# A new order of the steps in the cycle of the last part, on four engines

## What is computed

```python
# L3_xattn, for each of 64 sequences; x is layer-normed, textual = ctx (77 keys x 128)
txt_proj = textual @ Ws                     # 77 x 128
feat_proj = x @ W                           # 128 x 128
h = tanh(txt_proj[None] + feat_proj[:, None] + b)     # 128 tokens x 77 keys x 128
rho = h @ w + mask                          # 128 x 77
att = softmax(rho)
txt_h = att @ textual
out = tanh(txt_h @ Wcw.T + bcw) * x + tanh(txt_h @ Wcb.T + bcb)
# L3_ffn: each token to one of 8 experts, at most 1024 tokens for each, in order of tokens
probs = softmax(x @ wg); idx = argmax(probs)
locations = running count of the tokens of the same expert
mask = onehot(idx) * (locations < 1024)
out = gate * (x @ W[idx].T + b[idx])
```

## Time and profile before

| what | us |
|---|---|
| median of 3 runs (3680.53 to 3686.89) | 3683.99 |
| the profiled execution | 3685.05 |
| its span in the trace | 3683.3 |
| from 2708.45 to 3598.20, 56 turns of the last part | 889.75 |

### The profile page before, as it was taken

One profiled execution on the slowest core, in us unless ns is written; L12 is line 12 of the kernel. 1 busy time (PEld: TensorE's weight loads), 2 busy tenths in 40 slices (PEclk: granted clock), 3 DMA queues, 4 the chain that ended last, 5 costly groups with the idle time before them and its releaser, 6 DMA issues. The chain is left out here.

```text
span 3683.3 us, 79834 instructions
## 1 busy us (share of the span) xinstructions
PE 3112.4 (85%) x28490; PEld 2223.3 (60%) x28490; DVE 2687.1 (73%) x7707; ACT 2309.9 (63%) x6401; POOL 778.5 (21%) x1179
## 2 busy tenths in 40 slices
PE   6999999999997797899999949565388888888887
PEld 5666666666664465566666634225266676666675
DVE  2777777777774344788888856995578888888885
ACT  2889898989894353444444410420378888788885
POOL 0223232323232000233333300000122212222121
PEclk9999999999996898899999969777678888788887
DMA  1011111111110211011111100002100000000000
GB/s 40 19 32 32 31 31 32 31 32 30 33 32 13 74 43 37 19 28 28 28 28 28 26 16 0 0 0 72 31 10 12 13 13 13 13 12 13 13 13 8
DMA packets 173531, 90.21 MB, mean 24 GB/s; under 512 B 43971, under 2 KB 169541, under 8 KB 173156
## 3 DMA queue, kind: packets, MB, share of 16 engines
q1 hardware_dynamic: 160612, 72.67, 7.2%
q0 software_dynamic: 4096, 8.40, 0.7%
q10 hardware_dynamic: 8448, 4.20, 0.4%
HBM read 42.86 MB, written 42.34 MB: 23 GB/s over the span
## 5 line engine op out<-in xcount | busy, mean ns | idle before, releaser
L2149 DVE TENSOR_TENSOR th<-tf 128x2048 f32<-128x2048 f32 x256 | 584.9, 2287 | 45.5 <-PE p_rho L2051 37.9
L1996 ACT ACTIVATE th<-th 128x2048 f32<-128x2048 f32 x256 | 489.0, 1911 | 0.2 <-DVE th L2149 0.2
L2051 PE MATMUL p_rho<-th,w_row 128*32 128x128 f32 x8192 | 322.9, 307 | 56.6 <-ACT th L1996 56.6
L2051 PEld LDWEIGHTS p_rho<-th,w_row 128*32 128x32 f32 x8192 | 241.2, 122 | 96.4 <-ACT th L1996 63.2
L593 ACT ACTIVATE probf<-fs,colf 128x128 f32<-128x128 f32 x1024 | 277.9, 385 | 5.0 <-DVE colf L889 1.7
L564 ACT ACTIVATE prob<-prob,col 128x77 f32<-128x77 f32 x1024 | 269.8, 356 | 6.7 <-DVE col L844 6.6
L2007 ACT ACTIVATE tl<-tf 128x128 f32<-128x128 f32 x832 | 256.0, 395 | 0.0
L1662 PE MATMUL acc<-xnT_all,wT 128*128 x384 | 200.2, 686 | 60.9 <-ACT stage L1702 32.6
L1109 POOL TENSOR_TENSOR col<-col,minus_half 128x1 f32<-128x1 f32 x256 | 146.3, 578 | 488.1 <-DVE col L1381 351.8
L2112 PE MATMUL p_f<-w_exp,xm 128*128 128x128 f32 x1024 | 234.1, 421 | 0.0
L2112 PEld LDWEIGHTS p_f<-w_exp,xm 128*128 128x128 f32 x1024 | 217.6, 323 | 6.6
(11 more groups left out here) (419 smaller groups left out, 8079.9 us busy)
## 6 DMA issues: line engine op xcount, KB each, us to landing
rows<-zeros SPq DMA_DIRECT2D x64, 256.0 KB, 2.5
cxT<-in_ctxT SPq DMA_DIRECT2D x128, 38.5 KB, 2.0
xb<-rows SPq DMA_DIRECT2D x67, 64.0 KB, 1.8
rows<-yb SPq DMA_DIRECT2D x67, 64.0 KB, 1.6
x<-in_x SPq DMA_DIRECT2D x64, 64.0 KB, 1.8
x_mid<-x SPq DMA_DIRECT2D x64, 64.0 KB
z<-x_mid SPq DMA_DIRECT2D x64, 64.0 KB
x_next<-z SPq DMA_DIRECT2D x64, 64.0 KB, 1.5
```

What stands on the lines that cost most here:

```text
L1996: nc.scalar.activation(b[:], b[:], ACT.Tanh).then_inc(act_done, ACT_L.did(f"t{c}.tanh", e))
L2051: last = nc.tensor.matmul(p_rho[r][ROWS * b:ROWS * (b + 1), 0:TOK], w_row[:, ROWS - 1 - a:2 * ROWS - 1 - a], tanh[:, k, :], start=(a == 0) ...
L2149: nc.vector.tensor_tensor(th[i % NT][:], tf[s][:, n * KT:(n + 1) * KT].unsqueeze(2).to_broadcast([128, KT, TOK]), tf[s][:, FEAT:FEAT + TOK ...
```

## The change

Only the four strings are written anew. No instruction, tile, buffer or wait is added, removed or resized; each step keeps what it waits for. The order within a turn changes on all four engines, and the turn in which some steps are done: on PE the chunks r.rho0, r.rhoL and r.rho1 come one turn earlier (@1 instead of @2) and so does r.rho3 (@2 instead of @3), on ACT x3.exp goes from @3 to @2, t2 and t3 from @2 to @1, on DVE x3.x from @4 to @3. The expert steps f3.pick to f3.out keep their turn (@5).

```diff
 ACT_D = """
-    x3.exp@3 f3.kT@5 t3.tanh@2 x3.PT@3 t2.tanh@2 ta.tanh@1 f3.xT@4 t0.tanh@1 x3.xT x3.rho@2 f3.exp@4 x3.gate@3
-    tb.tanh@1 x3.proj t1.tanh@1
+    f3.kT@5 tb.tanh@1 x3.PT@3 t1.tanh@1 x3.rho@2 t0.tanh@1 x3.gate@3 x3.xT f3.xT@4 ta.tanh@1 f3.exp@4 x3.proj
+    t2.tanh@1 x3.exp@2 t3.tanh@1
 """
 DVE_D = """
-    x3.x@4 f3.pick@5 f3.taken@5 f3.stats@4 x3.stats f3.aggr@4 x3.aggr f3.keep@5 x3.sum0@1 f3.gate@5 f3.xm@5 x3.rden@3
-    x3.sum1@1 f3.out@5 x3.norm x3.gb@3 f3.norm@4 x3.sum2@1 f3.nmax@4 x3.sum3@1 f3.emax@4 x3.y@3 f3.rden@4 f3.eq@4
-    x3.nmax@2 f3.first@4
+    f3.pick@5 f3.taken@5 x3.sum0@1 f3.keep@5 f3.gate@5 x3.stats x3.sum1@1 x3.aggr f3.xm@5 x3.sum2@1 x3.norm x3.rden@3
+    f3.norm@4 x3.gb@3 f3.out@5 x3.sum3@1 f3.nmax@4 x3.y@3 x3.nmax@2 x3.x@3 f3.stats@3 f3.emax@4 f3.rden@4 f3.eq@4
+    f3.first@4 f3.aggr@3
 """
 PE_D = """
-    f3.T@5 r.rho3@3 f3.route@5 r.rho0@2 r.rhoT@3 x3.proj@1 r.rhoL@2 f3.place@5 f3.kT@5 p.PT@3 f3.g@5 r.rho1@2 p.gate@3
-    f3.y@5 r.rho2@2 x3.T
+    r.rho2@2 f3.kT@5 p.PT@3 f3.g@5 r.rho3@2 p.gate@3 f3.y@5 x3.T r.rhoT@2 f3.T@4 x3.proj f3.route@4 r.rho0@1 r.rhoL@1
+    r.rho1@1 f3.place@4
 """
 POOL_D = """
-    x3.rstd@1 f3.rstd@5 f3.eps@4 x3.eps
+    f3.rstd@4 x3.eps x3.rstd f3.eps@3
 """
```

## The result

| what | before, us | after, us |
|---|---|---|
| median (lowest to highest) | 3682.66 (3680.53 to 3686.89, 4 runs) | 3559.97 (3552.31 to 3561.23, 4 runs) |
| span of the profiled execution | 3683.3 | 3550.5 |
| mean granted clock over that span | 0.874 | 0.899 |

The ratio is 0.9661, with a 95% interval of 0.9644 to 0.9678. The new order saves 123 us, where 45 were predicted: faster as forecast, and faster than the range allowed (3570 to 3705). The profiled execution of after, 3552.31 us, lies 7.7 under its median.

A forecast was written before the change was run, and what follows sets the result against it. No engine filled the 15.89 us turn; the period was a full-clock cycle of about 13.5 us plus what TensorE's low clock takes. (15.89 - 15.1) x 57 = 45 us off 3683.99 gave 3640 us, range 3570 to 3705.

The forecast's parts named there:

- The cycle at full clock: Steady turn without low clock: VectorE bounds it at 13.25 us, 0.3 under the old turn, saving 17 us.
- What a pair of turns costs: A turn with a clock fall, 15.95 us, and the late turn after it, 14.95: together 30.9, a mean of 15.45.
- How often the clock falls: Steady turns: one full-clock turn to five in pairs with a fall, giving a mean of 15.1 us.
- the rival without falls: TensorE's clock never falls in steady turns: 13.25 us a turn, 3534 us in all; chance 0.05.
- the one with rare falls: The run rhoL, rho1, rho2 carries the clock on; one fall in five turns, 14.1 us each, 3582; chance 0.20.
- The first turns: The part's first turns, engines half empty, were left as they are, with no gain or cost counted.
- GpSimd at nothing: x3.eps and x3.rstd beside f3.xm end before sum2, f3.rstd runs beside sum0: cost nothing.
- The half microsecond by which `f3.rstd` might have held up sum0: If f3.rstd starts just ahead of sum0, it blocks the sum; left out, at full size some 28 us later.
- The slower rival: The late turn of a pair falls too, 17.65 us; in every second pair 3697, in every pair 3736; chance 0.19.
- the clock under 0.75: Sign over the steady stretch: a granted clock under 0.75 means the forecast fails high; 0.75 to 0.85 was expected.
- The mark that I had set for the forecast to fail low: Sign over the steady stretch: a granted clock above 0.9, where 0.75 to 0.85 was expected.

The follow-up runs named there:

- e2: New order with three zero-adding matmuls a turn, one ahead of TensorE's wait for f3.keep, two ahead of its wait for f3.kT: 3527.96 us.
- e6: Old order with one zero-adding matmul a turn, ahead of TensorE's wait for x3.exp: 3577.77 us.
- e3: New order with one TensorE step, r.rho3, moved behind f3.y: 3761.6 us.
- e9: New order with GpSimd's old order string put back: 3553.58 us.
- e4: Old order with four zero-adding matmuls a turn right behind f3.y, where TensorE never waits: 3764.05 us.

## Why the prediction was right and wrong

**The cycle at full clock: right.** 13.25 us forecast, 13.22 measured, with VectorE the bound and without a gap. The gain of the order itself, 0.3 a turn, is 0.31. Timeline of DVE in such a turn of after, across the places where gaps stood before:

```profile
2865.59 2.28 DVE L2149 TENSOR_TENSOR th<-tf 128x2048 f32<-128x2048 f32 x1
...
2868.49 0.34 DVE L2214 SCALAR_TENSOR_TENSOR x<-p_f,colf,x 128x128 f32<-128x128 f32 x1
2868.75 2.28 DVE L2149 TENSOR_TENSOR th<-tf 128x2048 f32<-128x2048 f32 x1
```

`f3.out` (L2214) no longer waits for `f3.y`. e2 bears it out: 13.22 in nearly every steady turn (three took 13.55 to 13.72).

**What a pair of turns costs: right in kind, 2.3 us too dear.** Forecast 15.95 + 14.95 = 30.9, measured 14.96 + 13.62 = 28.6. Three items. The wait before `f3.out` was 1.3 us, where 10.4 - 9.2 = 1.2 was forecast. Route ended 6.8 us behind the start of `f3.y` (2946.62 to 2953.45), where 14.25 - 6.6 = 7.65 was reckoned, since the five small steps behind `f3.y`, priced from single rows at 3.82 us, take 3.25 here (2950.20 to 2953.45), and `f3.y` 3.58 instead of 3.8; why the steps are shorter here than in the earlier trace rows, at the same low clock, isn't shown. So `f3.nmax` waited 0.5, not 1.4 or more. And the low clock ended earlier inside the run of chunks, with `rho0` at 1.94 but the second half of `rhoL` and `rho1` at full clock, so the next turn was late by 0.4 instead of 1.7. The steps through which it lasts, and where it ends, were as I wrote.

**How often the clock falls: the step that failed.** "With one full-clock turn to five in such pairs" the reckoning came to a mean of 15.1. Measured, up to about 3300, are four full-clock turns in seven, one pair, and a fall so short that it is over with `f3.y` (3.42 us instead of 2.05, a turn of 14.2), which I had not priced: a mean of 13.65. Had I taken the measured frequency with my own prices, (4 x 13.25 + 30.9 + 14.2) / 7 = 14.0 a turn, 3577. So 63 of the 80 us of the miss are the frequency, and the rest, to 3560, is about the size of the dearer pair (2.3 / 7 x 57 = 19 us). The argument in the prediction compared the waits of the new order (1.4 us in 3.5) with those of one falling turn, and gave less weight to the other half of its own sentence, that the old order has a wait of 0.84 us 5 us ahead and the new one has three chunks in one run there. That this run of three is what keeps the clock isn't shown: no run took it apart. The runs say that a small amount of work near the waits decides: one matmul of about 0.2 us in e6 takes 107 us off before, and one chunk moved in e3 costs 202, about half of it with the clock. With such steepness, and with two neighbouring turns of after that have the same waits to 0.03 us and the same 4.50 us of work and differ in the clock, a count of waits couldn't have told a fall in nearly every second turn from two in seven, one of them short. The range should have reached down to the rival without falls, 3534. The rival nearest to the result was the one with rare falls (0.20, 3582): it is what happened, with a cheaper pair.

**The first turns: a term left at nothing that costs 7 us.** I left them "as they are", since each engine is half empty there. But filling the part takes 49.9 us in the new order against 43.3.

**GpSimd at nothing: right.** Its order changes no time that the runs can tell (e9). Timeline of POOL, after:

```profile
2859.89 2.46 POOL L1950 TENSOR_TENSOR colf<-colf,minus_half 128x1 f32<-128x1 f32 x1
...
2864.96 0.57 POOL L1950 TENSOR_TENSOR col<-col,minus_half 128x1 f32<-128x1 f32 x1
```

`f3.rstd` beside a sum takes 2.46, `x3.rstd` beside `f3.xm` 0.57, as laid out. The half microsecond by which `f3.rstd` might have held up sum0, by the Trainium skill (SBUF — State Buffer, "Who interferes with whom"), isn't there: `x3.sum0` beside it starts at 2859.64, ahead of it, and takes 2.29 us, like every other (mean 2281 ns). By that rule the sum, being first, holds the ports, and the trace agrees: it is GpSimd's operation that takes longer. The other order came now and then, and there the sum's row isn't longer either. In this pair of rows of after GpSimd's operation starts 0.06 us ahead and lies beside the sum for 0.50 us, and the sum takes 2.29 us, not 2.8:

```profile
2886.34 0.57 POOL L1950 TENSOR_TENSOR colf<-colf,minus_half 128x1 f32<-128x1 f32 x1
...
2886.40 2.29 DVE L2149 TENSOR_TENSOR th<-tf 128x2048 f32<-128x2048 f32 x1 [0.24 <-issue]
```

By the rule it would have been blocked, so here the measurement differs from the page, and the measurement decides. A second pair, at 3324.08, reads the same. They are few, and spans on GpSimd are rough; what held the sum's start for 0.24 us isn't known.

**The rival without falls** didn't come: the clock fell in two turns of seven, as the earlier trace rows had argued. The rule of long single gaps (the Trainium skill, TensorE: Matmul & The Clock Gate, "HAM oscillation — how this bites in real kernels") is contradicted in after too: in the turn that lost the clock at 2945.8 the waits of the weak stretch are 0.22, 0.44, 0.28 and 0.44 us, as short as in the turn that kept it. The section behind it on that page ("A second HAM failure mode: psum-queue depth-cycling") has another case, short idles between groups of matmuls, and that is the one this kernel is like.

**The slower rival** didn't come: the late turn of a pair (13.62) kept the clock in the regular stretch up to 3300. Behind 3360 four turns in succession lost it, three of them behind a turn with a fall, but the four took 14.93, 14.89, 14.35 and 14.93 us, none near the 17.65 that I had priced. Nor was the clock under 0.75. The mark that I had set for the forecast to fail low, a granted clock above 0.9, is what happened (0.93 up to 3300, 0.91 over all 63 turns).

## What to carry to other kernels

Where TensorE isn't the bound but its steps are in the chain, look at its granted clock beside the turn before anything else, and find a turn at full clock and one without it: their difference is the price. Then try a few matmuls that add nothing (zeros into a sum that is open anyway) ahead of the waits of the weakest stretch, before orders are written anew; here four a turn gave 147 us on the old order and three gave 32 on the new, and the new order with fills, 3528, is the best of all that ran. When a forecast rests on how often the clock falls, let the range reach to "never" and to "always".

## What the runs showed of the hardware

- Tiny amounts of work at the right place hold TensorE's clock: one matmul of about 0.2 us in a turn of 15 took the clock from 0.83 to 0.95 between 2708 and 3500 (e6), and four at another place of the turn left it at 0.80 (e4).
- The same steps with the same waits, none above 0.5 us, keep the clock in some turns and lose it in others: 4.50 us of work in 5.70 stood ahead of both. In after this has a rhythm of seven turns, 95.6 us, up to about 3300, and then another with more falls; in e9, with the same order on TensorE, the pairs come every four to seven turns. What sets the rhythm, and why it changed, isn't settled; no run was made on it.
- A 128x1 operation of GpSimd takes 2.46 us beside a sum of VectorE with two operands in SBUF and 0.57 beside `f3.xm`, and VectorE's operation keeps its time in both. A sum that started 0.06 us behind such an operation kept its 2.29 us as well.
